# A two-branch layer on one core: half slices stacked, pointwise in split float32r, weight remainders on VectorE, and the order around the squares' transposes

## What is computed

```
xn = layernorm(x)
# branch s
a = pointwise(causal_dwconv3(rmsnorm(xn))) + b + xn      # 256x256
b = minGRU(rmsnorm(a)) + a                               # 256x512, scan over tokens
s = gelu(rmsnorm(b) @ w1.T + b1) @ w2.T + b2 + b         # 256x1024, 1024x256
# branch g: every operand rounded to 4-bit floats in blocks of 16
h = silu(fp4(xn) @ fp4(w_gate).T) * (fp4(xn) @ fp4(w_up).T)   # 704 columns each
g = silu(fp4(h) @ fp4(w_down).T)
out = x + s * g
```

## Time and profile before

| | before |
|---|---|
| runs | 1084.11, 1087.17, 1086.87 us; median 1086.87 |
| profiled execution | time 1085.26 us, span 1083.5 us |
| TensorE busy | 1061.8 us, 98% of the span |
| VectorE busy | 934.5 us, 86% |
| ScalarE busy | 607.3 us, 56% |
| GpSimd busy | 147.5 us, 14% |
| granted TensorE clock | 0.997 of full speed on average |

### The profile page before, as it was taken

One profiled execution on the slowest core, in us unless ns is written; L12 is line 12 of the kernel. 1 busy time (PEld: TensorE's weight loads), 2 busy tenths in 40 slices (PEclk: granted clock), 3 DMA queues, 4 the chain that ended last, 5 costly groups with the idle time before them and its releaser, 6 DMA issues. The chain is left out here.

```text
span 1083.5 us, 18319 instructions
## 1 busy us (share of the span) xinstructions
PE 1061.8 (98%) x6954; PEld 967.9 (89%) x6954; DVE 934.5 (86%) x1720; ACT 607.3 (56%) x967; POOL 147.5 (14%) x123
## 2 busy tenths in 40 slices
PE   7899999999999999999999999999999999999998
PEld 6788989989898998989999898998989899898998
DVE  6978988989888898988889898898989889898895
ACT  5564464564746547474654747455574645647452
POOL 1230101112020110201111010111101011120010
PEclk9999999999999999999999999999999999999999
DMA  7000001010010101001010010101001010100110
GB/s 248 1 21 1 1 2 59 1 60 1 1 59 1 59 1 47 13 2 59 1 60 1 21 40 1 59 1 60 1 1 59 1 59 1 59 1 2 39 40 21
DMA packets 29365, 31.45 MB, mean 29 GB/s; under 512 B 1120, under 2 KB 28512, under 8 KB 29280
## 3 DMA queue, kind: packets, MB, share of 16 engines
q1 hardware_dynamic: 28448, 29.43, 8.7%
q10 hardware_dynamic: 832, 0.87, 0.2%
HBM read 21.90 MB, written 8.39 MB: 28 GB/s over the span
## 5 line engine op out<-in xcount | busy, mean ns | idle before, releaser
L990 PE MATMUL gu_ps<-gu_hi,xq_hi 128*128 128x352 f32 x512 | 168.3, 329 | 0.0
L990 PE MATMUL gu_ps<-gu_lo,xq_hi 128*128 128x352 f32 x512 | 165.9, 324 | 0.0
L990 PE MATMUL gu_ps<-gu_hi,xq_lo 128*128 128x352 f32 x512 | 165.7, 324 | 0.0
L990 PE MATMUL w_ps<-w_hi,act_hi 128*128 128x256 f32 x480 | 140.1, 292 | 0.0
L990 PE MATMUL w_ps<-w_hi,act_lo 128*128 128x256 f32 x480 | 135.1, 281 | 0.0
L990 PE MATMUL w_ps<-w_lo,act_hi 128*128 128x256 f32 x480 | 134.9, 281 | 0.0
L990 PE MATMUL w_ps<-dn_hi,hqt_hi 128*128 128x256 f32 x384 | 116.6, 304 | 2.0 <-DVE hqt_lo L519 2.0
L990 PE MATMUL w_ps<-dn_hi,hqt_lo 128*128 128x256 f32 x384 | 108.5, 283 | 0.0
L990 PE MATMUL w_ps<-dn_lo,hqt_hi 128*128 128x256 f32 x384 | 108.4, 282 | 0.0
L818 ACT ACTIVATE g<-w_ps 128x256 f32<-128x256 f32 x64 | 24.7, 385 | 147.7 <-PE w_ps L990 147.6
L496 DVE TENSOR_TENSOR hid<-sl,gu_ps 128x704 f32<-128x704 f32 x64 | 56.8, 887 | 58.8 <-PE gu_ps L990 58.2
(11 more groups left out here) (136 smaller groups left out, 2703.6 us busy)
## 6 DMA issues: line engine op xcount, KB each, us to landing
x_in<-x_dram SPq DMA_DIRECT2D x16, 512.0 KB, 5.8
x_res<-x_dram SPq DMA_DIRECT2D x16, 512.0 KB, 5.0
out_dram<-o SPq DMA_DIRECT2D x15, 512.0 KB, 3.5
act<-w_t_dram SPq DMA_DIRECT2D x1, 1024.0 KB, 11.3
w_f<-w_t_dram SPq DMA_DIRECT2D x1, 1024.0 KB, 13.8
w_f<-w_down_dram SPq DMA_DIRECT2D x1, 704.0 KB, 9.4
hid<-w_gate_dram SPq DMA_DIRECT2D x1, 640.0 KB, 5.9
hid<-w_up_dram SPq DMA_DIRECT2D x1, 640.0 KB, 9.3
```

The source lines that it names most:

```text
L990: done = M.matmul(psum, l, r, start=first and i == 0, stop=last and i == len(terms) - 1)
```

## The change

- Half slices stacked: the sixth slice of the hidden columns holds the 64 half-slice columns twice (`fp4_hidden_values` writes them a second time in place of the zeros, for hidden rows and down weights). After the transposes partitions 64 to 127 of that slice are a twin of 0 to 63. `hidden_low` subtracts the first five slices into hqt_lo as before and overwrites the twin in hqt_hi with its own remainder. `down` then needs two products for the last slice: (high, low) against low weights and against high weights.
- `pointwise` takes y and its weights as float32r pairs: y_hi by ScalarE (`front_y_high`), y_lo by VectorE (`front_y_low`), in homes shared with keep and cand; all eight transposes come first, then twelve products.
- The low parts of w1 and w2 move from GpSimd to VectorE (`ff_low`); order and dummy matmuls of `first` are rearranged.
- `front_moments` is split: the statistics of chunk c + 2 at the end of body(c), the moments in the next body after the second `hidden_values`; SP loads x_in ahead of the store.
- TensorE: down(c - 1, 3) ahead of the squares' transposes, ff2(c - 1, 3) after them; the two transposes of x2b that open an ff2 are a function of their own.
- The batches of `gelus_low` are 4 and 4 in place of 5 and 3, and GpSimd's sum starts after the fourth.
- Last chunk: remainders of act ahead of the third rounding, GpSimd's sum after all eight, another order of down and ff2.

```diff
-        pw = sb("pw", [P, KD, D])
+        pw_hi = sb("pw_hi", [P, KD, D], F32R)
+        pw_lo = sb("pw_lo", [P, KD, D], F32R)
...
+        keep, y_hi = shared_home(("keep", [P, KD, L], F32), ("y_hi", [P, KD, L], F32R))
         take = xs
-        cand = sb("cand", [P, KD, L])
+        cand, y_lo = shared_home(("cand", [P, KD, L], F32), ("y_lo", [P, KD, L], F32R))
...
+                load(i + 3)
                 store(i)
-                load(i + 3)
...
-                if c < B - 2:
-                    pool.wait_ge(actlo_ready, KF * (c + 1) + 5)
+                pool.wait_ge(actlo_ready, KF * (c + 1) + (4 if c < B - 2 else KF))
...
+            def fp4_hidden_values(dst, rounded):
+
+                n, last = NBI * FP4_BLOCK, NFULL * P // FP4_BLOCK
+                fp4_values(dst[:, 0:n], NBI, rounded)
+                return V.scalar_tensor_tensor(blocks(dst[:, n:KI * P], NBI - last),
+                                              blocks(q_m[:, NFULL * P:n].bitcast(BF16), NBI - last),
+                                              1.0 / UNIT, spread(q_scale[:, last:NBI], NBI - last),
+                                              ALU.mult, ALU.mult)
...
+            def front_y_low(c):
+
+                for k in range(KD):
+                    dve.wait_ge(yhi_ready, KD * c + k + 1)
+                    V.tensor_tensor(y_lo[:, k, :], y[:, k, :], y_hi[:, k, :].bitcast(F32),
+                                    ALU.subtract).then_inc(ylo_ready, 1)
...
-                V.tensor_tensor(hqt_lo[:], hqt_ps, hqt_hi[:].bitcast(F32), ALU.subtract).then_inc(hqtlo_ready, 1)
+                V.tensor_tensor(hqt_lo[:], hqt_ps[:, 0:NFULL, :], hqt_hi[:, 0:NFULL, :].bitcast(F32), ALU.subtract)
+
+                twin = hqt_hi[LAST:P, NFULL, :]
+                V.tensor_tensor(twin, hqt_ps[LAST:P, NFULL, :], twin.bitcast(F32),
+                                ALU.subtract).then_inc(hqtlo_ready, 1)
...
+            def ff_low(j):
+
+                _, src, hi, lo = split_weights[j]
+                for k in range(KD):
+                    dve.wait_ge(whi_ready, KD * j + k + 1)
+                    V.tensor_tensor(lo[:, k, :], src[:, k, :], hi[:, k, :].bitcast(F32),
+                                    ALU.subtract).then_inc(flo_ready, 1)
...
             def body(c, front):
                 hidden_values(c - 1, 1, fp4_round(NBI, carried["ratios"]))
-                gelus_low(c - 1, range(5))
+                gelus_low(c - 1, range(4))
                 hidden(c, 0)
                 scales = hidden_scales(c - 1, 2)
                 add_squares(c * 2)
@@ -664,7 +708,9 @@
                 ratios = fp4_ratios(hid[:, 2, :], NBI, scales)
                 clamp_sums(c * 2, w_ps[:, 0, :])
                 hidden_values(c - 1, 2, fp4_round(NBI, ratios))
-                gelus_low(c - 1, range(5, KF))
+                if front and c > 1:
+                    front_moments(carried["stats"])
+                gelus_low(c - 1, range(4, KF))
                 hidden(c, 2)
                 scaled(c * 2, x1, w_ps[:, 1, :], (x1_ready, KD * (c + 1)))
                 scales = hidden_scales(c - 1, 3)
@@ -674,30 +720,34 @@
                 dve.wait_ge(dve_step, ratios)
                 hidden(c, 3)
                 hidden_values(c - 1, 3, fp4_round(NBI, ratios))
-                if front:
-                    front_moments(c + 1)
+                if front and c == 1:
+                    front_moments(front_stats(c + 1))
                 recurrence(c, 0)
                 recurrence(c, 1)
                 hidden_low(c - 1, 3)
                 add_squares(c * 2 + 1)
                 output(c - 1, 0, w_ps[:, 0, :])
-                clamp_sums(c * 2 + 1, gu_ps[:, 0, 0, :])
                 if front:
                     front_rows(c + 1)
+                clamp_sums(c * 2 + 1, gu_ps[:, 0, 0, :])
+                output(c - 1, 1, w_ps[:, 1, :])
                 scales = hidden_scales(c, 0)
                 scaled(c * 2 + 1, x1, gu_ps[:, 0, 1, :], (x2_ready, KD * (c + 1)))
                 scaled_low(c * 2 + 1)
-                output(c - 1, 1, w_ps[:, 1, :])
                 ratios = fp4_ratios(hid[:, 0, :], NBI, scales)
                 hidden_values(c, 0, fp4_round(NBI, ratios))
                 output(c - 1, 3, w_ps[:, 3, :])
                 output(c - 1, 2, w_ps[:, 2, :])
                 if front:
-                    front_fp4_values(c + 1, front_fp4_ratios(c + 1))
+                    ratios = front_fp4_ratios(c + 1)
                     front_taps(c + 1)
+                    front_fp4_values(c + 1, fp4_round(T * NBD, ratios))
+                    front_y_low(c + 1)
                     carried["ratios"] = fp4_ratios(hid[:, 1, :], NBI, hidden_scales(c, 1))
                     hidden_low(c, 0)
                     front_fp4_low(c + 1)
+                    if c + 2 < B:
+                        carried["stats"] = front_stats(c + 2)
 
...
-                ratios = fp4_ratios(hid[:, 2, :], NBI, hidden_scales(c, 2))
+                gelus_low(c, range(2))
                 hidden_low(c, 0)
-                rounded = fp4_round(NBI, ratios)
-                gelus_low(c, range(KF // 2))
-                hidden_values(c, 2, rounded)
-                gelus_low(c, range(KF // 2, KF))
+                gelus_low(c, range(2, KF))
+                scales = hidden_scales(c, 2)
                 hidden_low(c, 1)
+                hidden_values(c, 2, fp4_round(NBI, fp4_ratios(hid[:, 2, :], NBI, scales)))
                 ratios = fp4_ratios(hid[:, 3, :], NBI, hidden_scales(c, 3))
                 hidden_values(c, 3, fp4_round(NBI, ratios))
                 hidden_low(c, 2)
                 last_output(0)
+                last_output(1)
                 hidden_low(c, 3)
-                for t in range(1, T):
-                    last_output(t)
+                last_output(2)
+                last_output(3)
...
+            def front_y_high(c):
+
+                for k in range(KD):
+                    act.wait_ge(y_ready, KD * c + k + 1)
+                    act.wait_ge(pw_done, KD * c)
+                    act.wait_ge(x2_ready, KD * c)
+                    A.copy(y_hi[:, k, :], y[:, k, :]).then_inc(yhi_ready, 1)
...
+                gelus(c, (0,))
+                if front:
+                    front_y(c + 1)
+                gelus_high(c, (0,))
+                for j in range(1, KF // 2):
                     gelus(c, (j,))
                     gelus_high(c, (j,))
                 if front:
-                    front_y(c + 1)
-                    gelus(c, range(KF // 2, KF))
+                    gelus(c, range(KF // 2, KF - 2))
+                    front_y_high(c + 1)
+                    gelus(c, range(KF - 2, KF))
...
+                pe.wait_ge(y_ready, KD * (c + 1))
                 for e in range(KD):
-                    pe.wait_ge(y_ready, KD * (c + 1))
                     for t in range(T):
                         M.matmul(w_ps[:, e, t * P:(t + 1) * P], xn[:, t, e * P:(e + 1) * P], ident[:],
                                  is_transpose=True, start=t == 0, stop=False)
+                pe.wait_ge(yhi_ready, KD * (c + 1))
+                pe.wait_ge(ylo_ready, KD * (c + 1))
+                for e in range(KD):
                     for k in range(KD):
-                        last = product(w_ps[:, e, :], pw[:, k, e * P:(e + 1) * P], y[:, k, :], False, k == KD - 1)
+                        last = product(w_ps[:, e, :], (pw_hi[:, k, e * P:(e + 1) * P], pw_lo[:, k, e * P:(e + 1) * P]),
+                                       (y_hi[:, k, :], y_lo[:, k, :]), False, k == KD - 1)
...
-                for k in range(KI):
-                    last = product(bank[:, 0:D], (hqt_hi[:, k, :], hqt_lo[:, k, :]),
-                                   (dn_hi[:, k, :], dn_lo[:, k, :]), k == 0, k == KI - 1)
-                last.then_inc(dn_done, 1)
+                for k in range(NFULL):
+                    product(bank[:, 0:D], (hqt_hi[:, k, :], hqt_lo[:, k, :]), (dn_hi[:, k, :], dn_lo[:, k, :]),
+                            k == 0, False)
+
+                M.matmul(bank[:, 0:D], hqt_hi[:, NFULL, :], dn_lo[:, NFULL, :], start=False, stop=False)
+                M.matmul(bank[:, 0:D], hqt_hi[:, NFULL, :], dn_hi[:, NFULL, :], start=False,
+                         stop=True).then_inc(dn_done, 1)
...
-                ff2(c - 1, 0, w_ps[:, 0, :], (ss_ready, 2 * c + 1))
-                ff2(c - 1, 1, w_ps[:, 1, :], (xs_ready, KD * (2 * c + 1)))
+                ff2_open(c - 1, 0, w_ps[:, 0, :], (ss_ready, 2 * c + 1))
+                ff2_open(c - 1, 1, w_ps[:, 1, :], (xs_ready, KD * (2 * c + 1)))
+                ff2(c - 1, 0, w_ps[:, 0, :])
+                ff2(c - 1, 1, w_ps[:, 1, :])
+                down(c - 1, 3)
                 sum_squares(c * 2 + 1, gu_ps[:, 0, 0, :], (coef_ready, KD * c + 1))
-                down(c - 1, 3)
+                ff2_open(c - 1, 3, w_ps[:, 3, :], (hqtlo_ready, T * c))
+                ff2(c - 1, 3, w_ps[:, 3, :])
```

(32 more changed lines are left out.)

221 lines of the change are left out of this document (118 added, 103 removed).

## The result

The changed kernel takes **1080.3 us** (median of 4, 1079.55 to 1081.26) against 1086.86 before (1084.11 to 1087.17, 4 runs beside it): ratio 0.9942, interval 0.9925 to 0.9959. That is 6.6 us less. Forecast were 1073.5 and 13.4 less. The sign is right, the gain is half of what I had; 1080.3 lies in the range of 1061 to 1086. The profiled execution has a span of 1078.0 and a time of 1079.83.

What follows compares the result with a forecast made beforehand. TensorE (98% busy) bounds the kernel, with VectorE late at two downs: 63.55 us a chunk. Beginning -6.0, chunk 1 -1.7, thirteen middle chunks at -0.42, last -0.2: -13.4 us, to 1073.5; 8-in-10 range 1061 to 1086.

Steps and rivals of the forecast that it cites:

- What goes on TensorE: Middle chunks: savings of 0.65, 0.47 and 0.49 us take a chunk from 63.99 to 62.4 if nothing is late.
- split pointwise: TensorE, pointwise: twelve float32r products in place of four float32 ones save 0.65 us a chunk.
- half slices: TensorE, down: the last slice needs two products in place of three, four times a chunk, saving 0.47 us.
- order of down: TensorE: down(c-1, 3) moved ahead of sum_squares, ff2 filling the gap, removes the 0.49 us wait before the second spread.
- Which waits come: TensorE waits for VectorE at down(c-1, 1), 0.3 us, and down(c-1, 2), 0.84 us, in middle chunks.
- q_wide under the sum: VectorE, early in the chunk: q_wide overlaps GpSimd's output sum and loses 0.85 us.
- Moments on the path: VectorE: the moments add 0.55 us to the chain that down(c-1, 2) waits for.
- The twin of hidden_low (128 columns) costs 0.29: VectorE, hidden_low: first part shrinks by 0.13, neighbours overlap by 0.08, so the remainder is ready only 0.08 us later.
- rival (c): VectorE: twin and successor lose 0.08 us overlap each, three twins on the late path; +0.4 a chunk, 1079.2 us; 22%.
- (a): Rival: GpSimd's sum does not bite, VectorE being half a microsecond earlier; 63.24 a chunk, 19.2 us saved, 1067.7; 17%.
- (b): Rival: TensorE stays the only bound, no wait anywhere; 62.4 a chunk, 31.5 us saved, 1055.4; 7%.
- recurrence's products 35.95 to about 36.1: Chunk 0: start of the recurrence's products, old to new, in a beginning forecast 6.0 us shorter.

Runs made afterwards that it cites:

- e13: e8 with xq of chunk 0 ahead of the taps and one act_lo moved behind the fourth hidden_values, ahead of the recurrence; 1057.27 us.
- e11: e8 with the stacked half slices undone (no twin, no copy, 18 products per down); 1066.55 us.
- e12: e8 with the old order of down(c-1, 3) and ff2(c-1, 3) put back; 1075.7 us.
- e1: Changed kernel with the twin subtraction of hidden_low on partitions 0 to 63 in place of 64 to 127; 1070.13 us.
- e9: Changed kernel with xq of chunk 0 made ahead of the taps again, as before the change; 1078.98 us.
- e3: Changed kernel with the pointwise product back to float32, without y_hi, y_lo, pw_hi and pw_lo; 1080.88 us.
- e7: Changed kernel with GpSimd's two remainders of the recurrence's weights narrowed to 16 of 512 columns; 1078.66 us.
- e6: Changed kernel with GpSimd's whole output sum moved beside VectorE's xq_lo and statistics, except in the last two chunks; 1072.82 us.
- e8: Changed kernel with the twin at partition 0, the moments ahead of the recurrence and the output sum moved as in e6; 1063.29 us.

## Why the prediction was right and wrong

**What goes on TensorE: right in total.** I had 62.4 us a chunk if nothing is late; e13 shows 62.40. Single terms, each read in the relieved kernel: split pointwise 0.62 (0.65), half slices 0.56 (0.47; e11, without a wait, against e13, 62.96 less 62.40), order of down 0.74 (0.49). Part of the last is that the new order of front_rows makes the old place of down dearer than it was before: in e12 the squares' sum starts on VectorE only as front_rows ends (519.59), and from the recurrence's first product to the second spread are 15.53 us, where before had 15.43. The three terms add up to 1.92 where 1.58 went, so the exact total does not check each of them.

**Which waits come: right; their sizes: too small.** Both downs, with hidden_low as releaser, in chunks 2 to 14; smaller in chunk 1 (0.30) and with a wait of 1.11 in the last (forecast 1.2). As delays of TensorE I had 0.3 and 0.85; measured are 0.54 and 0.99. That is the 0.4 a chunk between 63.55 and 63.96. q_wide under the sum: 0.76 lost (0.85). Moments on the path: 0.56 (0.55).

**The step that failed in the middle chunks: "The twin of hidden_low (128 columns) costs 0.29, while the first part shrinks by 0.13: the remainder is ready 0.08 later with the 0.08 overlap of neighbours".** The overlap is not there. From hqt_lo to the operation behind hidden_low are 0.81 us before (the earlier trace rows has that hqt_lo at 506.61; xs_lo follows at 507.42) and 1.10 after: 0.29 more, not 0.08. Without the hold (e1) it is 0.87, about what I had. So each twin is about 0.23 dearer, and three lie on the late path: 0.65 a chunk by e1. This is rival (c), which I priced at 0.4 a chunk (its own terms, six times 0.08, are 0.48) and gave 22%. That its period, 63.55 + 0.4 = 63.95, is the measured 63.96 is in part luck, as the next paragraph shows. The Trainium skill (VectorE: DVE Perf Modes, "Two Vector instructions with no wait between them") says that an operation whose output starts in another quadrant of the partitions than the last one waits until all earlier ones have finished, and so does the next one that goes back; the rows of the changed kernel and of e1 agree with it, 0.10 and 0.13 us. I had quoted the rule in the prediction and yet built the sum on the rows of operations that all start at partition 0: the trace of before had no case, and I took the absence of a case for the likelier price.

The rest of the sum was not exact either, only hidden: without the hold (e1) the period is 63.31, 0.24 below my 63.55, since the wait at down(c-1, 1) goes there altogether. So a hold priced 0.25 too low and a sum 0.24 too high met in 63.95. In the rivals, the 19.2 and 31.5 us of (a) and (b) are more than their middle chunks with my terms for the rest give (17.5 and 28.4); the prediction doesn't list what makes up the difference.

**The step that failed in the beginning: the milestone "recurrence's products 35.95 to about 36.1".** The walk counted what VectorE adds (pw_lo, y_lo) and left out that the change turns xq and the taps round, and that TensorE's pointwise(0) is queued behind the transposes of xq. That is 1.9 us by e9 (1.3 by its median). The marks behind it keep the distance: first DVE step 41.85 (forecast 39.8), first ff1 56.71 (54.5), gate_up of chunk 0 71.44 (69.2). Only then comes more, 2.9 at the start of chunk 1 (97.4 forecast, 100.32). There TensorE waits 0.84 us for y_lo at pointwise(1), at 97.45, where I had y_lo ready 0.9 ahead. No run took that wait away by itself; e3, which has no y_lo, needs 61.33 us from the recurrence's products to chunk 1 in place of 62.17. GpSimd's remainder, which I first held responsible (e7), accounts for 0.5 at most.

The total missed by 6.8 us on the medians. In the profiled pair it is 7.9: the middle chunks lack 5.3, the beginning 2.9 and chunk 1 0.1, and the last chunk gives 0.4 more than I had.

**What the split of the sum hid.** The forecast adds parts. The experiments show that the same part is worth 0 or 0.62 (pointwise) and -0.44 or +0.21 (half slices) a chunk, by whether VectorE is late. With the waits in place, what is taken from TensorE only lengthens the wait. The two waits are worth 1.56 a chunk in the changed kernel, 20 us over thirteen chunks.

**Open.** Why undoing the order of down costs 0.74 where its listed wait and the 0.16 beside it give 0.65 was not taken apart. The beginning differs by 0.9 us between traces whose chunk 0 is the same (e7), so that effects under 1 us there are not shown by one trace.

## What to carry to other kernels

When work moves from the bounding engine to one that is 86% busy, read for each handover how early the second engine is, and count the added operations on that path alone: here 0.32 us of slack decided over some 20 us. Price an added small operation by the distance from neighbour to neighbour, not by its duration, and look at which partition it starts before taking that distance from other rows. Moving three cheap things off the late path (an operation to partition 0, the moments into idle time, GpSimd's sum beside operations that read PSUM) turned 0.6% into 2.1%, and two more such moves into 2.6%.

## What the runs showed of the hardware

**The start partition costs time.** An operation of VectorE on partitions 64 to 127 between two that start at partition 0: 0.10 us later, and its successor 0.13 later, than the same operation on partitions 0 to 63 (changed kernel and e1, four places in each of thirteen chunks).

**GpSimd holds only some operations of VectorE.** Under a GpSimd operation that reads SBUF, q_wide (128x44, SBUF to SBUF) took 0.95 us (1.74 in the last chunk) in place of 0.19, xq (two SBUF inputs) 1.91 in place of 1.22, two y_lo 2.36 in place of 1.29; two xq_lo with one input in PSUM 1.29 and four statistics 1.40, both unchanged (e6). The Trainium skill (SBUF — State Buffer, "Who interferes with whom") says that GpSimd and VectorE share one pair of ports by an exclusive lock, and that only operations of VectorE that need the second port meet it; these rows agree.

**The granted clock after the same wait.** In chunk 0 TensorE waits 2.91 us for xq in e6 and in e8. In e8 the granted clock stays at 1.00 (2.4 GHz); in e6 it is 0.58 in 22 to 24 and 0.57 in 24 to 26 (means of stretches of which most lies at the lower of the two levels, 1.2 GHz), and the recurrence's products start 1.81 later (40.25 against 38.44, of which 0.18 was there before the fall). e12, with 2.92, fell too. The other three executions of e6 show a mean granted clock of 1.000 and take 1072.18 to 1072.92, this one 0.998 and 1074.88: the same kernel goes either way. Rows of e6, TensorE alone:

```profile
22.00:24.00 2.00, 2.00 (x13) 0.58 0.05 16
24.00:26.00 2.00, 2.00 (x12) 0.57 0.00 0
```

The changed kernel, whose wait there is 1.69, kept 1.00. A beginning that differs by 2 us between two kernels with the same middle is therefore read from this row before it is put down to an edit.
